# Adding up a node's counts where two groups of edges share it: TensorE products against GpSimd copies, and the order of the first loads, in a three-pass graph network kernel

## The chip, the cores and the metric

One core of one Trainium2 chip. The metric is the device time of one execution in microseconds (us). The kernel before takes 331.2 us, the median of 3 runs (330.82 to 331.33).

## What is computed

A graph of 3125 nodes with 128 features, and 53,125 edges `src -> dst` sorted by `dst`, each with one of 64 relation types. Three passes over the same edges, each of them a mean over the edges that end in a node:

```python
deg = segment_sum(ones, dst)
# 1: relation layer
msg = (x[src] + rel_emb[type]) @ W_msg.T + b_msg
x1  = layernorm(x + x @ W_self.T + b_self + segment_sum(msg, dst) / max(deg, 1))
# 2, 3: two SAGE layers
agg(h) = segment_sum(h[src], dst) / max(deg, 1)
h   = swish(agg(x1) @ W1_l.T + b1 + x1 @ W1_r.T)
out = layernorm(x1 + agg(h) @ W2_l.T + b2 + h @ W2_r.T)
```

## The kernel before

**The matrix of counts.** All three passes multiply node rows by one matrix `A` (`counts`), kept in SBUF as float16: 25 blocks of 128 source nodes (partitions) by 3150 target columns. The last block also holds, in its upper 64 partitions, how often each relation type ends in a node. Once `A` is there, each sum over edges is a row of dense products. The features are split into a high and a low float16 part, so that each block costs two products.

**Building it (the loop over groups).** The edges are cut into 416 tiles of 128, four tiles to a group, 104 groups. As the edges are sorted, a group touches a window of at most 38 columns, from its first target (`base`) on. For each group:

- VectorE writes the one-hot rows of the four tiles into one of three slots (L1386 for source row and type, L1393 for block and column), and every fourth group the rows for the types (`window_hot`, L1378) and for the node that is shared with the next group (`next_hot`, L1373). It may reuse a slot only when TensorE has counted the group three before (`released`).
- TensorE (`count`, L993) multiplies them into two PSUM banks, one for each half of the blocks: 8 products of 132 or 143 columns (L999) and 4 for the types (L1006). Two windows (`RING`) alternate, four banks in all.
- Two neighbouring groups mostly share a node: the last target of one is the first column of the next. The copy of the next window into `A` would overwrite that column. So TensorE multiplies the last tile of a group a second time into column 0 of the *next* window: `share(0)`, `share(1)` (L1016) and one product for the types (L1036), three for each group but the last. `share` waits until ScalarE has copied the group before out of that bank.
- ScalarE copies each half of the window to `A[:, half, base:base+38]` (L941), at an address from a register that it loads for eight groups at a time. A copy waits for the count and for the copy of the group before, since windows overlap.

**Work that rides along.** After the count of a group, TensorE does what is due by a table written out by hand: `project` (L1040, the nodes times `W_msg`, chunk c of 512 nodes after group `PROJECTED[c]`), `own` (L1121, the nodes times `W_self`, after the groups in `OWN`), and products of the first pass (`aggregate_tile`, L1079) for tiles of 128 nodes whose columns are complete. `spread()` deals these out: 13 products of 128 columns to a group, 16 up to group 15, 8 in the last four, none in groups of `OWN`, beginning with group `SUMS_FROM`. ScalarE and VectorE turn projected chunks into the two parts of the table (`high_bits` L854, `low_bits` L1403), and do the layer norm of finished chunks in turns spread over groups. VectorE also prepares the lists of groups 16 to 103 (`other_span`) between groups 8 and 15: eleven operations on 352 or 87 columns.

**Before the loop.** SyncE issues the loads of the edge lists (`dst`, `src`, for groups 0 to 15, then for 16 to 103), ScalarE those of `first_dst` and `type`. SyncE then waits for all targets before it issues `w_msg`, the biases and `x_turned` in three pieces (`CUTS`, chunks 0-1, 2-3, 4-6). TensorE runs 7 products on constants that nobody reads (`UNREAD`, L1186), then group 0.

**After it.** The rest of pass 1, then passes 2 and 3 by chunks of 512 nodes: 50 (or 49) products of 512 columns (L1101), `messages` (L1155), `own_later` (L1174), and the steps of ScalarE and VectorE behind them. The last chunk of pass 3 is one tile of 128 nodes. Its end is a chain: `lead` (L864), `messages`, `add_last` (L1480), `measure`, `combine`, `root`, `invert`, `normalise`, store. `keep_own` (L907) stands behind `root` of the chunk before on ScalarE. GpSimd writes constants at the start (L804 to L824) and then has nothing to do. Later, VectorE checks that the input meets the limits on which windows rely (`check_edges`), and a flag sends the rare other inputs to a slow general path.

## Time and profile before

| | us |
|---|---|
| median of 3 runs (range) | 331.2 (330.82 to 331.33) |
| the profiled execution | 331.4 |
| its span in the profile | 329.6 |
| loop over groups, first product to last | about 7.5 to 163.9 |
| rest of pass 1 | to about 175 |
| passes 2 and 3 | to about 327 |
| the last store | to the end |

The profile gives busy time of each engine, the chain of work that ended last, the costliest groups of instructions with their mean duration, and the order of instructions in time. VectorE, ScalarE and GpSimd instructions overlap with the next of the same engine by their last stretch, and TensorE's overlap far more: what one costs there is the step from its start to the next start, not its duration.

### The profile page before, as it was taken

The page shows a single profiled execution, that of the slowest core. Times are in us where ns is not written, and L with a number is a line of the kernel's source. Part 1 is how long each engine was busy: PE and PEld are TensorE (multiplying, and loading weights), DVE is VectorE, ACT ScalarE, POOL GpSimd, SP SyncE. Part 2 cuts the span into 40 slices and gives each one's busy share as a digit, 9 for nine tenths or more (in the row PEclk, how much of TensorE's full clock was granted, in tenths as well). Part 3 has the DMA queues.
Part 4 walks back from the last instruction along what each step waited for, and adds up shares of the span by engine and source line. Part 5 has one row for each costly group of instructions (what it writes and reads, how often), then busy time and mean ns, then how long its engine had stood idle before and what let it go on. Part 6 is the DMA issues. An engine that isn't in the chain of part 4 may idle for free.

```text
span 329.6 us, 10324 instructions
## 1 busy us (share of the span) xinstructions
PE 318.8 (97%) x3880; PEld 246.1 (75%) x3880; DVE 232.0 (70%) x632; ACT 167.4 (51%) x370; POOL 4.8 (1%) x20
## 2 busy tenths in 40 slices
PE   4899999999999999999999999999999999999994
PEld 1799999999999999999984554554564545545663
DVE  7699999999999999999777864314318246145154
ACT  4588777789789789788722322312322311211212
POOL 5000000000000000000000000000000000000000
PEclk9799999999999999999999999999999999999999
DMA  3500000000000000000011111111011112221111
GB/s 116 211 3 3 4 2 7 6 2 12 3 2 11 3 4 10 3 4 9 5 51 31 24 26 28 24 27 25 16 22 30 21 27 58 52 56 28 32 45 37
DMA packets 22087, 8.88 MB, mean 27 GB/s; under 512 B 16671, under 2 KB 21652, under 8 KB 22036
## 3 DMA queue, kind: packets, MB, share of 16 engines
q1 hardware_dynamic: 21460, 7.75, 9.6%
q8 instruction: 35, 0.57, 0.7%
q10 hardware_dynamic: 576, 0.43, 0.4%
q14 instruction: 16, 0.13, 0.1%
HBM read 3.02 MB, written 1.60 MB: 14 GB/s over the span
## 4 chain that ended last, share of the span: by engine, by line
PE 94%; DMA 3%; DVE 1%; SPq 1%; issue 0%; ACT 0%; DVEq 0%
PE ps L1101 39%; PE ps L1079 21%; PE ps L999 20%; PE ps L1174 4%; PE ps L1155 4%; PE ps L1051 2%; PE ps L1131 2%; PE ps L1006 1%; DMA counts<-dst_t 1%; DMA table<-x_turned 1%; PE ps L1016 1%; PE ps L1036 0%; DVE stats L1504 0%; PE ps L1115 0%; DVE new_first L1532 0%
## 5 line engine op out<-in xcount | busy, mean ns | idle before, releaser
L1101 PE MATMUL ps<-counts,table 128*128 128x512 f16 (+3 forms) x785 | 134.0, 329 | 0.0
L941 ACT CAST counts<-ps 128x494 f32 x208 | 107.0, 573 | 26.4 <-PE ps L999 25.6
L1101 PEld LDWEIGHTS ps<-counts,table 128*128 128x128 f16 x785 | 63.9, 97 | 65.1 <-issue 0.4
L1079 PE MATMUL ps<-table,counts 128*128 128x128 f16 x1200 | 81.9, 218 | 0.0
L1079 PEld LDWEIGHTS ps<-table,counts 128*128 128x128 f16 x1200 | 67.9, 97 | 0.0
L999 PE MATMUL ps<-hot 128*128 128x143 f16 (+1 forms) x560 | 60.2, 232 | 0.3 <-DVE hot L1393 0.3
L1393 DVE TENSOR_TENSOR hot<-iota,edges 128x1100 f16<-128x1100 f16 x70 | 50.5, 722 | 0.0
L999 PEld LDWEIGHTS ps<-hot 128*128 128x128 f16 x560 | 48.0, 100 | 2.3 <-DVE hot L1393 1.2
L1386 DVE TENSOR_TENSOR hot<-iota,edge_rows 128x768 f16<-128x768 f16 x70 | 38.4, 548 | 1.5 <-PE ps L1036 0.7
L1006 PE MATMUL ps<-window_hot,hot 128*128 128x19 f16 x280 | 38.8, 178 | 0.0
L884 ACT ACTIVATE scaled<-ps,rdeg 128x128 f32<-128x128 f32 (+1 forms) x74 | 21.4, 372 | 22.0 <-PE ps L1155 22.0
L1497 DVE TENSOR_TENSOR new_first<-ps,scaled 128x512 f32<-128x512 f32 (+2 forms) x9 | 5.7, 628 | 37.9 <-ACT scaled L884 37.9
L999 PE MATMUL ps<-room 128*128 128x132 f16 (+1 forms) x272 | 28.8, 231 | 0.0
L1006 PEld LDWEIGHTS ps<-window_hot,hot 128*128 128x128 f16 x280 | 27.4, 99 | 0.1
L1393 DVE TENSOR_TENSOR room<-iota,edges 128x1100 f16<-128x1100 f16 x34 | 24.6, 723 | 0.0
L1497 DVE TENSOR_TENSOR hot<-ps,scaled 128x512 f32<-128x512 f32 (+1 forms) x8 | 4.7, 583 | 27.5 <-ACT scaled L884 27.5
L999 PEld LDWEIGHTS ps<-room 128*128 128x128 f16 x272 | 23.5, 101 | 0.0
L864 ACT COPY room<-ps 128x512 f32<-128x512 f32 (+2 forms) x8 | 4.2, 524 | 32.5 <-PE ps L1101 32.4
L1016 PE MATMUL ps<-next_hot,hot 128*128 128x13 f16 (+1 forms) x138 | 19.4, 180 | 0.0
L1386 DVE TENSOR_TENSOR room<-iota,edge_rows 128x768 f16<-128x768 f16 x34 | 18.6, 548 | 0.3 <-PE ps L1036 0.2
L1006 PE MATMUL ps<-window_hot,room 128*128 128x19 f16 x136 | 18.8, 178 | 0.0
L864 ACT COPY hot<-ps 128x512 f32<-128x512 f32 (+2 forms) x8 | 3.6, 450 | 26.4 <-PE ps L1101 26.4
(146 smaller groups left out, 320.0 us busy)
## 6 DMA issues: line engine op xcount, KB each, us to landing
table<-x_turned SPq DMA_DIRECT2D x2, 512.0 KB, 4.3
edge_rows<-table SPq DMA_TRANSPOSE x54, 2.3
out<-new_first SPq DMA_DIRECT2D x3, 256.0 KB, 2.5
table<-x_turned SPq DMA_DIRECT2D x1, 576.0 KB, 5.7
out<-hot SPq DMA_DIRECT2D x2, 256.0 KB
window_hot<-table SPq DMA_TRANSPOSE x23, 2.4
iota<-table SPq DMA_TRANSPOSE x21, 2.3
counts<-counts SPq DMA_DIRECT2D x6, 53.0 KB
```

Source lines behind the costliest of these rows:

```text
L884: last = nc.scalar.activation(scaled[0:part, t], ps[0:part, bank, t * D:(t + 1) * D], ACT.Copy, scale=rdeg[0:part, tile:tile + 1])
L941: nc.scalar.copy(A[:, HALVES[half], bass.ds(bases[group % 8], GROUP_W)], window(group, half)).then_inc(copied[half], 1)
L999: return nc.tensor.matmul(window(group, half)[:, :, at[t]], row(tiles[t], LOW_AT, P), blocks_of(tiles[t], half), start=group == half == t ...
L1006: return nc.tensor.matmul(relations(group)[:, column], row(tiles[t], TYPE_AT, P), window_hot[:, group // NEXT % 2, tiles[t] // PAIR % (NEX ...
L1016: nc.tensor.matmul(window(then, half)[:, :, 0:1], row(tiles[-1], LOW_AT, P), next_hot[:, group // NEXT % 2, HALVES[half], group % NEXT].un ...
L1079: last = nc.tensor.matmul(ps[:, sums_bank(q), at:at + P], A[:, b, tile * P:(tile + 1) * P], table0[:, b, which, :], start=k == at == 0, st ...
L1101: last = nc.tensor.matmul(ps[:, sums_bank(q), 0:nodes], table[:, b, which, :], A[:, b, at:at + nodes], start=b == which == 0, stop=b + 1 = ...
L1155: sent = nc.tensor.matmul(ps[0:size, messages_bank(q), t * D:(t + 1) * D], sum_T(q)[:, at], weight(layer, 0), start=True, stop=True)
L1174: last = nc.tensor.matmul(to, x_T(q)[:, at], weight(layer, 1), start=q == EARLY and t == 0, stop=False, skip_group_check=True)
L1386: nc.vector.tensor_tensor(rows[:, :, TYPE_AT + REL_ROW:M_AT, :].rearrange("p h (k c) t -> p h k c t", c=PIECE), iota[:, 0:PIECE, :].unsque ...
L1393: nc.vector.tensor_tensor(rows[:, :, M_AT:M_AT + TILE_C, :], iota[:].unsqueeze(1).to_broadcast([P, PAIRS, TILE_C, PAIR]), edge[:, PLACED, ...
L1497: nc.vector.tensor_tensor(rows(new(q), q), from_own, rows(scaled, q), ALU.add).then_inc(y_ready, 1)
```

## The change

- GpSimd takes over the shared node. For each group from 1 on and each half it **saves** column `base` of `A` into `carried` before ScalarE's copy of that group overwrites it (`save`), and **adds** it back after (`add_carried`): four operations for each group, of 13 or 12 elements in each partition, with the address from a register (9 loaded at a time). ScalarE's copy now waits for `saved` instead of its own copy before. The products of the first pass wait for the additions too (`wait_shared`).
- TensorE's three products for the shared node go, with `next_hot`, `next_node` and `next_block` on VectorE. Count of group g now waits, ahead of its first product of each half, for the copies of group g-2. VectorE's slots come free with `counted[1]`.
- The first loads change order: lists of groups 0 to 15, `w_msg`, `x_turned` (pieces of chunks 0, 1-2, 3-6), biases, then the lists of groups 16 to 103, all on SyncE without the wait. ScalarE keeps the types of groups 16 to 103 after group 8 instead of ahead of the loop.
- `project(0)` goes ahead of group 0, the other chunks, the owns, the low bits and the first products of pass 1 come one group earlier, and 5 unread products stand in place of 7.
- At the end `keep_own` goes ahead of `root`, and the last of the three tiles of the chunk before is normalised by VectorE while it would wait for the last square root. The last chunk has its own column of the statistics for that.

The diff, cut to its core:

```diff
-PROJECTED = (1, 1, 2, 3, 4, 5, 6)
+PROJECTED = (-1, 0, 1, 2, 3, 4, 5)
 PROJECTED_BANKS = (4, 5, 6, 7)
-LOWS = {3: 0, 4: 1, 5: 2, 6: 3, 7: 4, 8: 5, 9: 6}
+LOWS = {2: 0, 3: 1, 4: 2, 5: 3, 6: 4, 7: 5, 8: 6}
 TURNING = 20
-CUTS = (0, 2, 4, 7)
-OWN = (7, 9, 11, 12, 14)
+CUTS = (0, 1, 3, 7)
+OWN = (6, 8, 10, 11, 13)
 OWN_BANKS = (7, 7, 6, 7, 6)
-SUMS_FROM, EARLY_STEPS = 8, 15
+SUMS_FROM, EARLY_STEPS = 7, 15
...
+OTHER_TYPES = 8
 LISTED = (slice(0, FIRST * GROUP), slice(FIRST * GROUP, TILES))
-UNREAD = 7
+UNREAD = 5
...
+        def wait_shared(eng, groups):
+            for half in range(2):
+                eng.wait_ge(copied[half], groups)
+                eng.wait_ge(shared[half], groups - 1)
...
-            for part, span in enumerate(LISTED):
-                sp.dma_start(dst_i[:, span], dst_t[:, span]).then_inc(dst_in[part], 16)
-                sp.dma_start(src_i[:, span], src_t[:, span]).then_inc(src_in[part], 16)
-            sp.wait_ge(dst_in[1], 32)
+            sp.dma_start(dst_i[:, LISTED[0]], dst_t[:, LISTED[0]]).then_inc(dst_in[0], 16)
+            sp.dma_start(src_i[:, LISTED[0]], src_t[:, LISTED[0]]).then_inc(src_in[0], 16)
             sp.dma_start(weights_first[:, 0, :], w_msg).then_inc(message_weights_in, 16)
-            for k, b in enumerate((b_self, b_msg)):
...
             for k, piece in enumerate(x_in):
                 span = slice(CUTS[k] * CHUNK, min(CUTS[k + 1] * CHUNK, BLOCKS * P))
                 sp.dma_start(stage[:, span], x_turned[:, span]).then_inc(piece, 16)
+            for k, b in enumerate((b_self, b_msg)):
+                sp.dma_start(bias_first[k:k + 1, 0, :], b).then_inc(biases_in, 16)
+            sp.dma_start(dst_i[:, LISTED[1]], dst_t[:, LISTED[1]]).then_inc(dst_in[1], 16)
+            others = slice(LISTED[1].start + GROUP, TILES)
+            sp.dma_start(first_i[:, others], first_dst[others].partition_broadcast(P)
+                         ).then_inc(dst_in[1], 16)
+            sp.dma_start(src_i[:, LISTED[1]], src_t[:, LISTED[1]]).then_inc(src_in[1], 16)
+            sp.dma_start(type_i[:, LISTED[1]], type_t[:, LISTED[1]]).then_inc(type_in[1], 16)
             sp.dma_start(weights_first[:, 1, :], w_self).then_inc(weights_in, 16)
             sp.dma_start(bias_first[:, 1, :], b1.rearrange("o d -> (o d)").partition_broadcast(P)
...
+            def node_of(column, half):
+                return A[:, HALVES[half], bass.ds(column, 1)]
+            def save(group, half, column):
+                pool.wait_ge(copied[half], group)
+                if half == 1 and group > 1:
+                    pool.wait_ge(shared[0], group - 1)
+                elif half == 1:
+                    pool.wait_ge(saved[0], group)
+                elif group > 2:
+                    pool.wait_ge(shared[1], group - 2)
+                elif group > 1:
+                    pool.wait_ge(saved[1], group - 1)
+                nc.gpsimd.tensor_copy(carried[:, group % 2, HALVES[half]].unsqueeze(2),
+                                      node_of(column, half)).then_inc(saved[half], 1)
+            def add_carried(group, half, column):
+                pool.wait_ge(copied[half], group + 1)
+                if group + 1 < GROUPS:
+                    pool.wait_ge(saved[half], group + 1)
+                elif half == 0:
+                    pool.wait_ge(shared[1], group - 1)
+                else:
+                    pool.wait_ge(shared[0], group)
+                node = node_of(column, half)
+                nc.gpsimd.tensor_tensor(node, node, carried[:, group % 2, HALVES[half]].unsqueeze(2),
+                                        ALU.add).then_inc(shared[half], 1)
+            pool.wait_ge(constants, 16)
+            pool.wait_ge(base_ready, 1)
+            for group in range(1, GROUPS):
+                if group == FIRST:
+                    pool.wait_ge(base_ready, 2)
+                if group % 8 == 1:
+                    begin = group - 1
+                    bases = nc.values_load_multi_w_load_instructions(
+                        base_i[0:1, begin:min(begin + 9, GROUPS)],
+                        engines=[mybir.EngineType.Pool], min_val=0, max_val=LAST_BASE,
+                        skip_runtime_bounds_check_because="they have been clipped")[1]
+                for half in range(2):
+                    save(group, half, bases[group - begin])
+                    if group > 1:
+                        add_carried(group - 1, half, bases[group - 1 - begin])
+            for half in range(2):
+                add_carried(GROUPS - 1, half, bases[GROUPS - 1 - begin])
             general_gpsimd(pool)
         @block.scalar
         def _(act):
-            for part, span in enumerate(LISTED):
-                begun = slice(span.start + GROUP * part, min(span.stop + GROUP, TILES))
-                act.dma_start(first_i[:, begun], first_dst[begun].partition_broadcast(P)
-                              ).then_inc(dst_in[part], 16)
-                act.dma_start(type_i[:, span], type_t[:, span]).then_inc(type_in[part], 16)
+            begun = slice(0, LISTED[0].stop + GROUP)
+            act.dma_start(first_i[:, begun], first_dst[begun].partition_broadcast(P)
+                          ).then_inc(dst_in[0], 16)
+            act.dma_start(type_i[:, LISTED[0]], type_t[:, LISTED[0]]).then_inc(type_in[0], 16)
...
-            for part, span in enumerate(LISTED):
+            def keep_types(part, span):
...
+                if 0 < q < ALL_CHUNKS - 1:
                     act.wait_ge(rows_ready, q)
-                nc.scalar.activation(std[0:part, 0:tiles_of(q)],
-                                     moments[0:part, 0:tiles_of(q), 1],
+                nc.scalar.activation(std[0:part, columns(q)], moments[0:part, columns(q), 1],
                                      ACT.Sqrt, bias=eps_col[0:part]).then_inc(std_ready, 1)
...
-                        act.wait_ge(copied[half], group)
+                        act.wait_ge(saved[half], group)
                     nc.scalar.copy(A[:, HALVES[half], bass.ds(bases[group % 8], GROUP_W)],
                                    window(group, half)).then_inc(copied[half], 1)
-                for c in range(CHUNKS):
+                for c in range(1, CHUNKS):
                     if PROJECTED[c] == group:
                         high_bits(c)
+                if group == OTHER_TYPES:
+                    keep_types(1, LISTED[1])
...
+                if q + 1 == ALL_CHUNKS:
+                    keep_own(q)
                 if layer_of(q - 1) == 1:
                     gate(q - 1)
                 else:
                     root(q - 1)
                 if layer_of(q - 1) < 2:
                     high(q - 1)
-                if q + 1 == ALL_CHUNKS:
-                    keep_own(q)
                 if ahead:
...
-                def share(half):
-                    if group:
-                        pe.wait_ge(copied[half], group)
-                    nc.tensor.matmul(
-                        window(then, half)[:, :, 0:1], row(tiles[-1], LOW_AT, P),
-                        next_hot[:, group // NEXT % 2, HALVES[half], group % NEXT].unsqueeze(2),
-                        start=True, stop=False, skip_group_check=True)
                 pe.wait_ge(v_hot, group + 1)
+                if group >= RING:
+                    pe.wait_ge(copied[0], group - RING + 1)
                 for t in range(GROUP):
                     last = blocks(0, t)
+                    if t == 0 and group >= RING:
+                        pe.wait_ge(copied[1], group - RING + 1)
                     if t + 1 < GROUP:
                         types(t)
...
-                if not ends:
-                    share(0)
                 blocks(1, 3).then_inc(counted[1], 1)
-                if not ends:
-                    share(1)
-                    nc.tensor.matmul(relations(then)[:, 0:1], row(tiles[-1], TYPE_AT, P),
-                                     next_node[:, group:group + 1], start=False, stop=False,
-                                     skip_group_check=True).then_inc(released, 1)
...
-                        wait_copied(pe, READY[tile])
+                        wait_shared(pe, READY[tile])
...
                         skip_runtime_bounds_check_because="they have been clipped")[1]
+                if group == 0:
+                    project(0)
                 mine = group % LOADED * GROUP
                 count(group, places[mine + 1:mine + GROUP])
-                for c in range(CHUNKS):
+                for c in range(1, CHUNKS):
                     if PROJECTED[c] == group:
                         project(c)
                 if group in OWN:
...
                 if group >= SLOTS:
-                    dve.wait_ge(released, group - SLOTS + 1)
+                    dve.wait_ge(counted[1], group - SLOTS + 1)
                 if group % NEXT == 0:
                     if group >= 2 * NEXT:
-                        dve.wait_ge(released, group - NEXT)
-                    nc.vector.tensor_tensor(
-                        next_hot[:, group // NEXT % 2],
-                        iota[:, P:P + BLOCKS, 0:1].to_broadcast([P, BLOCKS, NEXT]),
-                        next_block[:, group:group + NEXT].unsqueeze(1).to_broadcast(
-                            [P, BLOCKS, NEXT]), ALU.is_equal)
+                        dve.wait_ge(counted[1], group - NEXT)
...
                 dve.wait_ge(ln_step, 3 * normalised(q) + 1)
-                if q:
+                if 0 < q < ALL_CHUNKS - 1:
                     dve.wait_ge(rows_ready, q)
...
                     combine(q)
+                    if q + 1 == ALL_CHUNKS:
+                        normalise(q - 1, [tiles_of(q - 1) - 1])
                     invert(q)
-                    normalise(q, range(tiles_of(q)))
+                    normalise(q, range(tiles_of(q) - (q + 2 == ALL_CHUNKS)))
                 if layer_of(q) < 2:
```

## Rows read from the trace of the kernel before

**Rows 1.** The page: busy time, and the chain that ended last by engine.
```profile
PE 318.8 (97%) x3880; PEld 246.1 (75%) x3880; DVE 232.0 (70%) x632; ACT 167.4 (51%) x370; POOL 4.8 (1%) x20
...
PE 94%; DMA 3%; DVE 1%; SPq 1%; issue 0%; ACT 0%; DVEq 0%
```

**Rows 2.** Windows, the head and groups 17 to 99; clock, DMA share, GB/s last.
```profile
12.00:16.00 4.00, 4.00 (x33) 3.94 (x33) 2.48 (x6) 1.95 (x4) 0.00 (x0) 0.63 0.31 113
...
38.14:158.82 120.68, 120.65 (x2308) 119.58 (x2306) 115.72 (x275) 98.39 (x211) 0.00 (x0) 1.00 0.02 5
```

**Rows 3.** Timeline of TensorE: ends of groups 16, 98 and 99 (start, duration, what).
```profile
38.14 0.16 PE L1036 MATMUL ps<-next_node,hot 128*128 128x1 f16 x1
...
157.20 0.23 PE L999 MATMUL ps<-room 128*128 128x132 f16 x1
...
157.29 0.23 PE L999 MATMUL ps<-room 128*128 128x132 f16 x1
...
157.41 0.89 PE L1079 MATMUL ps<-table,counts 128*128 128x128 f16 x13
...
158.82 0.16 PE L1036 MATMUL ps<-next_node,hot 128*128 128x1 f16 x1
```

**Rows 4.** Timeline of VectorE in groups that nothing else interrupts.
```profile
66.66 0.55 DVE L1386 TENSOR_TENSOR room<-iota,edge_rows 128x768 f16<-128x768 f16 x1
67.12 0.72 DVE L1393 TENSOR_TENSOR room<-iota,edges 128x1100 f16<-128x1100 f16 x1
67.77 0.55 DVE L1386 TENSOR_TENSOR hot<-iota,edge_rows 128x768 f16<-128x768 f16 x1
...
68.96 0.23 DVE L1373 TENSOR_TENSOR next_hot<-iota,next_block 128x100 f16<-128x100 f16 x1
69.11 0.30 DVE L1378 TENSOR_TENSOR window_hot<-iota_type,edges 128x304 f16<-128x304 f16 x1
```

**Rows 5.** Timeline of the head: GpSimd's operations, and VectorE's beside them.
```profile
4.41 0.23 DVE L1282 TENSOR_TENSOR counts<-counts,base 128x64 int32<-128x64 int32 x1
...
4.60 0.10 POOL L814 MEMSET small<- 128x1 f32 x1
4.63 0.12 POOL L815 MEMSET degree<- 128x25 f32 x1
...
4.96 0.29 POOL L818 TENSOR_SCALAR_AFFINE_SELECT new_first<-new_first 128x128 f32<-128x128 f32 x1 [0.16 <-POOL peaks L816]
4.99 0.34 DVE L1310 TENSOR_TENSOR counts<-edges,place 128x64 int32<-128x64 f16 x1
```

**Rows 6.** Timeline of ScalarE: copies of two windows.
```profile
65.82 1.01 ACT L941 CAST counts<-ps 128x494 f32 x2 [0.42 <-PE ps L999]
```

**Rows 7.** Timeline of the head: unread products, first one-hots, wait for chunks 0 and 1.
```profile
4.06 3.17 PE L1186 MATMUL ps<-iota 128*128 128x512 f16 x7 [4.06 <-POOL iota L805]
...
6.28 0.55 DVE L1386 TENSOR_TENSOR hot<-iota,edge_rows 128x768 f16<-128x768 f16 x1
...
7.53 0.31 PE L999 MATMUL ps<-hot 128*128 128x143 f16 x1 [0.30 <-DVE hot L1393]
...
11.15 3.41 PE L1051 MATMUL ps<-weights_first,table 128*128 128x128 f32 x16 [1.46 <-DMA table<-x_turned]
```

**Rows 8.** Timeline of TensorE: chunk 3 projected at full clock.
```profile
17.03 1.14 PE L1051 MATMUL ps<-weights_first,table 128*128 128x128 f32 x8
```

**Rows 9.** Groups by line, VectorE, 16 to 38 us: low bits, first and last list operation.
```profile
L1403 DVE SCALAR_TENSOR_TENSOR table<-ps,table 128x512 f16<-128x512 f32 (+1 forms) x6 | 3.7, 614 | 0.0
...
L1282 DVE TENSOR_TENSOR counts<-counts,base 128x352 int32<-128x352 int32 x1 | 0.5, 518 | 0.0
...
L1278 DVE TENSOR_SCALAR base<-counts 128x87 int32<-128x87 int32 x1 | 0.2, 229 | 0.0
```

**Rows 10.** DMA issues: KB each, median us from issue to landing.
```profile
table<-x_turned SPq DMA_DIRECT2D x2, 512.0 KB, 4.3
```

**Rows 11.** Timeline of the end: ScalarE's copy ahead of the last chunk's messages.
```profile
324.37 0.27 ACT L864 COPY hot<-ps 128x128 f32<-128x128 f32 x1
```

67 lines of the change are left out of this document (24 added, 43 removed).

## The prediction

> **What bounds the kernel now.** I read the busy times and the chain first. TensorE is busy 97% of the span and 94% of the chain [rows 1]. The others only matter where they could take its place. The change touches the loop over groups, so next I read windows of it. Over 83 groups TensorE works 120.65 of 120.68 us, VectorE 115.72, ScalarE 98.39 and GpSimd nothing [rows 2]. So TensorE bounds the loop, but VectorE is only 4% behind it, and that decides this case. One group takes (158.82 - 38.14) / 83 = 1.454 us from the end of group 16 to that of 99 [rows 3]. VectorE, with its busy time taken whole, needs at most 115.72 / 83 = 1.394.
>
> In the head the bound is something else. TensorE stands still for 1.46 us until chunks 0 and 1 of `x_turned` arrive, and then works 3.41 us on 16 products [rows 7] that take about 2.1 at full clock (8 take 1.14, the run-out of the last among it, [rows 8]). The granted clock of 12 to 16 us is 0.63 of the full 2.4 GHz [rows 2], so part of that stretch ran at 1.2 GHz, behind that idle time.
>
> **1. TensorE's three products go.** A product costs the step to the next start. From L999 to L999 with a `share` between them it is 0.09 us, and from L999 over `share(1)` and L1036 to the first L1079 0.12 [rows 3]. Without them each is one step of 0.06, what a product of 132 columns leaves until the next start. That saves 0.03 + 0.06 = 0.09 a group. A group would take 1.454 - 0.09 = 1.365. The wait that comes in their place, for the copy of group g-2 at the start of group g, asks for less than `share` did: the same copy was due before the last product of group g-1, and now also the products of pass 1 lie in front of it. Price 0.
>
> **2. VectorE loses `next_hot`.** It costs 69.11 - 68.96 = 0.15 us in every fourth group [rows 4], 0.04 a group. VectorE then needs at most 1.394 - 0.04 = 1.357. The true need is some hundredths lower, since the busy time holds the last 0.08 of each operation, in which the next could have started (0.55 against a step of 0.46, [rows 4]). So VectorE's margin to TensorE's 1.365 is 0.01 to 0.05 us a group, and each of the four new GpSimd operations may delay it by about 0.01 before VectorE is the bound.
>
> **3. GpSimd's four operations a group.** GpSimd itself has time. The loop shows none of its operations, the head does: small memsets start 0.03 apart and last 0.10 to 0.12, one that reads and writes 128 columns lasts 0.29 [rows 5]. Four such, each behind a semaphore, make 0.5 to 1.2 us of 1.365. The register load for eight groups is one more stop in eight groups; it can run while GpSimd waits for ScalarE.
>
> ScalarE waits for `saved` in place of `copied`. Its two copies take 1.01 together and it stood idle 0.42 before them [rows 6]. The save of one half has the 0.5 us of the other half's copy to hide in. What is queued behind a late save is `add_carried` and the save of the other half, and who would wait is ScalarE's next copy, then TensorE's count two groups on. Behind 0.5 of cover and 0.4 of idle time I price it at 0. If the cover is gone, each half shows what a save is longer than 0.5.
>
> What it costs VectorE is the open term. Call it d for each operation. **Lower end: 0.** VectorE's step is 0.65 for 1100 columns and 0.46 for 768 [rows 4], so 0.19 / 332 = 0.57 ns a column, and 0.02 of each step (up to 0.07 with the rounding of these starts) is not for columns. A read of 13 elements may fit there. A gain is excluded, as GpSimd takes nothing from VectorE but the small `next_hot`, already counted. **Upper end: 0.11.** At 4.99 us L1310 took 0.34, where L1282 of as many columns took 0.23, and the one GpSimd operation that reads SBUF ran beside it, 4.96 to 5.25 [rows 5]. So a delay of VectorE behind GpSimd does exist here. That operation reads 128 columns, the new ones 13, and VectorE was let go about when it ended. I take d = 0.01: nearest in elements is the small memset, which leaves its engine after 0.03 [rows 5], and part of that falls into the free stretch of a step. Price in the loop: none while 4 x 0.01 fits the margin.
>
> The Trainium skill speaks against this change. "SBUF — State Buffer", section "Who interferes with whom", says that a VectorE instruction with two SBUF inputs contends with a GpSimd instruction that reads SBUF, and that the lock lasts for the whole instruction, whoever comes first. The L1310 row agrees in its direction; by that rule the sum would come out as the second rival below has it.
>
> **4. The head.** `project(0)` (about 1.0 us, [rows 8]) moves to where TensorE waits for the first one-hots. Five unread products of 0.45 end at 6.3, the first count started at 7.53 [rows 7]. It needs `w_msg` and one chunk of `x_turned`, issued at about 2 us instead of 7. The idle 1.46 goes, and the 1.3 that the low clock cost in 3.41. Together TensorE would save 3.8 us, more with 17 groups of 0.09, less 16 products of pass 1 that come earlier (0.9). VectorE is slower than that. From its first L1386, now at 6.28 [rows 7], 0.3 earlier without `next_hot` and two list operations, it has 17 groups of 1.11 (67.77 - 66.66, [rows 4]), five `window_hot` of 0.22, seven low bits of 0.6 or less and nine list operations from 0.5 to 0.2 [rows 9], in all 18.9 + 1.1 + 4.0 + 3.2 = 27.2 us, so group 16 is ready at 33.3, counted at 34.0. I add 0.8 for waits between the two and 0.7 for 17 x 4 x 0.01. So group 16 ends at 35.5 where it ended at 38.14 [rows 3]: **-2.6**. Bounds: 0 if the loads come late, -4.1 if VectorE never waits.
>
> The moved loads: SyncE issues all of them, past one wait less. The lists of groups 16 to 103 now stand behind 1.6 MB of `x_turned`, but VectorE wants them in group 8, near 20 us. `w_self` stands last and is wanted in group 4. The types' two operations on ScalarE move into its idle time in group 8. Price 0 each.
>
> **5. The loop from group 17 on.** 87 groups less 0.09: **-7.7**. VectorE does chunk work in bursts, with three slots to even them out, and the margin is thin. I give back **+1.0** (0 to 3).
>
> **6. The end.** ScalarE's `lead` of the last chunk started at 324.37 behind `keep_own` [rows 11] and would start about 0.1 earlier, and one tile less stands ahead of `add_last` on VectorE. Each is a step on the last chain: **-0.2**. The store of the chunk before goes out some tenths later, still ahead of the last store.
>
> **Sum**, against the profiled execution's own 331.4 (span 329.6 and 1.8 around it; the median of the runs is 331.2, 0.2 lower): 331.4 - 2.6 - 7.7 + 1.0 - 0.2 = 321.9, and **322.0** for the median as far as this can tell.
>
> **Rivals.**
> *d near 0.03, about even.* VectorE becomes the bound. With d = 0.024, (1.454 - 1.357) / 4, the loop is as long as before. At 0.035, the memsets' distance, it is 1.497 x 87, +3.7, and the head -3.3 + 2.4: 331.4 + 3.7 - 0.9 - 0.2 = 334. This holds 326 to 336, either side of no change.
> *Slower: VectorE and GpSimd take turns at SBUF.* One mechanism, at L1386 and L1393: each reads two inputs from SBUF, and GpSimd's save or add holds it off, or waits itself until it ends and lets ScalarE's next copy wait. It decides from d = 0.024 on. At 0.06, half of what L1310 lost, a group takes 1.60: 87 x 0.14 + 0.8 - 0.2 gives 344. At 0.11, 1.80: 87 x 0.34 + 4.2 gives 365. I would expect 350. For it: L1310, and that VectorE is busy nearly always, so that no operation of GpSimd can avoid it. Against it: 13 elements are a tenth of what that row read.
> *The loads don't come in time.* `x_turned` took 4.3 us from issue [rows 10] for two chunks. If one chunk came after 6.3, TensorE would idle and again run at 1.2 GHz, and the head would give nothing: 325.
>
> **Chances.** Forecast 0.48, even 0.20 (0.08 faster, 0.04 the same, 0.08 slower), turns 0.25, late loads 0.07. "Same" is within 0.2%, 0.7 us, about what a measurement of this kernel can tell. That makes faster 0.63, same 0.04, slower 0.33. The range: from 318.5 (head -4.1, nothing given back, VectorE at its lower need) over the even case to 344, the near end of the turns. The forecast's own range is 319 to 325.
>
> **What would show it.** Right: a group from 17 to 99 takes 1.36 to 1.39, no row of L1016, L1036 or L1373, VectorE near 97% busy, L1386 still 0.55 and L1393 still 0.72, no TensorE wait for L941 or GpSimd, no low clock in the head. Wrong: L1386 or L1393 longer than before, or steps between them longer, TensorE waiting for VectorE's one-hots (d over 0.01), GpSimd's operations lasting many tenths, ScalarE's copies waiting for GpSimd. The head is wrong if TensorE waits for `x_turned` or shows 1.2 GHz after 7.5 us.

## The result, and the profile after

The changed kernel takes **398.8 us** (median of 4 runs, 397.98 to 399.01), against 331.3 before: a ratio of 1.2035, 95% interval 1.1997 to 1.2073. It is 67.5 us slower. I had forecast 322, with 344 as the upper end. Medians in this text are over all runs of a kernel; ratios and their intervals leave out the few executions that stood more than 1.5% above the fastest of the same kernel.

The page of the changed kernel, busy time, the chain that ended last by engine, and ScalarE's copies; then GpSimd's two groups in the loop (42 to 221 us):

```profile
PE 350.3 (88%) x3569; PEld 258.0 (65%) x3569; DVE 233.3 (59%) x601; ACT 177.4 (45%) x370; POOL 143.0 (36%) x432
...
PE 41%; POOL 35%; issue 16%; POOLq 6%; DVE 1%; ACT 0%; DVEq 0%; ACTq 0%
...
L1005 ACT CAST counts<-ps 128x494 f32 x208 | 117.6, 568 | 87.0 <-POOL carried L855 79.2
```
```profile
L868 POOL TENSOR_TENSOR counts<-counts,carried 128x12 f16 (+1 forms) x166 | 62.0, 374 | 26.9 <-POOL carried L855 5.5
L855 POOL COPY carried<-counts 128x13 f16 (+1 forms) x165 | 49.2, 298 | 40.9 <-POOL counts L868 40.9
```

Before, the chain was 94% TensorE [rows 1]. Now GpSimd, its sequencer and "issue" hold 57% of it. ScalarE stood idle 79 us in all behind the saves (L855). In the loop GpSimd's 62.0 + 49.2 us of work and 26.9 + 40.9 us between its own operations make 179.0 of 179 us: it never waits for anybody else there, and its own chain is the bound. VectorE is busy as long as before, over a longer span: it is not what got slower.

Windows of the changed kernel: the loop, its last part, and what follows (clock, DMA share, GB/s last):

```profile
38.00:200.00 162.00, 134.83 (x1836) 117.40 (x1837) 103.94 (x227) 95.59 (x188) 101.19 (x301) 0.96 0.01 4
200.00:230.00 30.00, 24.46 (x346) 22.55 (x343) 18.06 (x40) 18.06 (x37) 18.11 (x58) 0.89 0.01 4
230.00:396.00 166.00, 160.07 (x1068) 91.51 (x1065) 78.31 (x260) 40.20 (x104) 1.21 (x6) 0.99 0.15 33
```

I time the loop by where the last product of a group's count starts (L1064 here). Group 16 is there at 41.02 us (38.03 before), group 99 at 221.38 (158.73). A group takes 2.173 us instead of 1.454, 83 x 0.719 = 59.7 us more. The rest of the 65.2 by which group 103 is late is the head's 3.0 and 2.5 in the last four groups. Behind the loop it needs 1.4 us more (167.1 against 165.7 from group 103 to the end). The granted clock is 0.96 and 0.89 of full in the windows where TensorE is busy 83% and 82%. As GpSimd's chain has no pause in the loop, that clock doesn't set the pace there.

GpSimd's timeline in the loop, where nothing holds it up and where VectorE does:

```profile
101.19 0.20 POOL L855 COPY carried<-counts 128x13 f16 x1 [0.22 <-POOL counts L868]
101.54 0.24 POOL L868 TENSOR_TENSOR counts<-counts,carried 128x13 f16 x1
102.01 0.20 POOL L855 COPY carried<-counts 128x12 f16 x1 [0.23 <-POOL counts L868]
102.35 0.25 POOL L868 TENSOR_TENSOR counts<-counts,carried 128x12 f16 x1
102.83 0.20 POOL L855 COPY carried<-counts 128x13 f16 x1 [0.22 <-POOL counts L868]
...
105.51 0.60 POOL L868 TENSOR_TENSOR counts<-counts,carried 128x13 f16 x1
```

From 101.19 to 102.83 four operations take 1.64 us with VectorE out of the way. That is one group, and already more than the 1.454 of a group before. 0.20 and 0.25 of each pair is work, 0.15 and 0.22 is the way from the end of one operation over its semaphore to the start of the next. Ahead of each save it holds an operation on the address register (FUSED_REGOPS, 0.046). Where the addresses are fixed (e5 below), the same two ways take 0.08 and 0.13. The add at 105.51 takes 0.60, as VectorE's L1412 runs from 105.46.

VectorE beside them, the groups of the loop (42 to 221 us):

```profile
L1419 DVE TENSOR_TENSOR hot<-iota,edges 128x1100 f16<-128x1100 f16 x55 | 40.3, 732 | 0.0
L1412 DVE TENSOR_TENSOR hot<-iota,edge_rows 128x768 f16<-128x768 f16 x54 | 30.1, 557 | 19.0 <-PE ps L1064 18.9
```

0.732 and 0.557 stand against 0.72 and 0.55 [rows 4]: VectorE lost 0.01 an operation, and waits for TensorE.

### The profile page after: what moved, and what is told of

It is laid out like the page before. It is cut to its first block, busy times and chain, and to the rows that moved or that the text cites. A ratio compares the mean times of both kernels' runs of the same rounds, so it can differ in the third digit from the quotient of the medians.

```text
span 396.2 us, 10862 instructions
## 1 busy us (share of the span) xinstructions
PE 350.3 (88%) x3569; PEld 258.0 (65%) x3569; DVE 233.3 (59%) x601; ACT 177.4 (45%) x370; POOL 143.0 (36%) x432
## 4 chain that ended last, share of the span: by engine, by line
PE 41%; POOL 35%; issue 16%; POOLq 6%; DVE 1%; ACT 0%; DVEq 0%; ACTq 0%
PE ps L1154 33%; POOL counts L868 18%; POOL carried L855 16%; PE ps L1227 3%; PE ps L1208 3%; POOLq L855 2%; POOLq L878 2%; POOLq L862 1%; POOL iota L819 1%; PE ps L1132 1%; PE ps L1104 1%; PE ps L1239 1%; POOLq L852 0%; POOLq L848 0%; POOLq L868 0%
## 5 line engine op out<-in xcount | busy, mean ns | idle before, releaser
L1005 ACT CAST counts<-ps 128x494 f32 x208 | 117.6, 568 | 87.0 <-POOL carried L855 79.2
L1132 PE MATMUL ps<-table,counts 128*128 128x128 f16 x1200 | 87.6, 227 | 6.8 <-ACT counts L1005 4.1
L868 POOL TENSOR_TENSOR counts<-counts,carried 128x13 f16 x206 | 76.8, 373 | 33.4 <-POOL carried L855 6.7
L1132 PEld LDWEIGHTS ps<-table,counts 128*128 128x128 f16 x1200 | 75.7, 102 | 9.4 <-ACT counts L1005 4.1
L855 POOL COPY carried<-counts 128x13 f16 x206 | 61.2, 297 | 54.8 <-POOL counts L868 49.9
L1064 PE MATMUL ps<-hot 128*128 128x143 f16 (+1 forms) x560 | 73.9, 242 | 2.1 <-DVE hot L1419 0.9
L1071 PE MATMUL ps<-window_hot,hot 128*128 128x19 f16 x280 | 44.8, 182 | 17.4 <-ACT counts L1005 17.0
L1064 PEld LDWEIGHTS ps<-hot 128*128 128x128 f16 x560 | 49.6, 101 | 8.0 <-DVE hot L1419 2.0
L1412 DVE TENSOR_TENSOR hot<-iota,edge_rows 128x768 f16<-128x768 f16 x70 | 39.0, 557 | 21.9 <-PE ps L1064 21.6
L1064 PE MATMUL ps<-room 128*128 128x132 f16 (+1 forms) x272 | 36.4, 247 | 0.6 <-DVE hot L1419 0.4
L1071 PE MATMUL ps<-window_hot,room 128*128 128x19 f16 x136 | 22.1, 186 | 8.8 <-ACT counts L1005 8.5
L1064 PEld LDWEIGHTS ps<-room 128*128 128x128 f16 x272 | 24.5, 104 | 3.3 <-issue 0.7
L1412 DVE TENSOR_TENSOR room<-iota,edge_rows 128x768 f16<-128x768 f16 x34 | 18.9, 557 | 11.4 <-PE ps L1064 11.4
L1071 PEld LDWEIGHTS ps<-window_hot,room 128*128 128x128 f16 x136 | 14.0, 103 | 12.4 <-ACT counts L1005 12.1
```

What stands on the lines that cost most here:

```text
L855: nc.gpsimd.tensor_copy(carried[:, group % 2, HALVES[half]].unsqueeze(2), node_of(column, half)).then_inc(saved[half], 1)
L868: nc.gpsimd.tensor_tensor(node, node, carried[:, group % 2, HALVES[half]].unsqueeze(2), ALU.add).then_inc(shared[half], 1)
L1005: nc.scalar.copy(A[:, HALVES[half], bass.ds(bases[group % 8], GROUP_W)], window(group, half)).then_inc(copied[half], 1)
L1064: return nc.tensor.matmul(window(group, half)[:, :, at[t]], row(tiles[t], LOW_AT, P), blocks_of(tiles[t], half), start=half == t == 0, sto ...
L1071: return nc.tensor.matmul(relations(group)[:, column], row(tiles[t], TYPE_AT, P), window_hot[:, group // NEXT % 2, tiles[t] // PAIR % (NEX ...
L1132: last = nc.tensor.matmul(ps[:, sums_bank(q), at:at + P], A[:, b, tile * P:(tile + 1) * P], table0[:, b, which, :], start=k == at == 0, st ...
```

## The experiments

Two theories. **A:** GpSimd's four operations are one serial chain of 1.64 us a group, on which ScalarE's next copy hangs. VectorE's one-hots make it longer. **B:** taking turns with VectorE at SBUF is the loss. "Loop" is a group from 16 to 99 as above, in the profiled execution; "save" and "add" are the mean durations in the loop (of the operations in their place for e5 and e8, of 25 elements for e6's add). e2, e7, e8, e9 and e11 were run once each.

| kernel | time, us | loop, us | save, add, us |
|---|---|---|---|
| before | 331.3 | 1.454 | |
| changed | 398.8 | 2.173 | 0.298, 0.374 |
| e1 rest only | 328.8 | 1.455 | |
| e2 no one-hots | 360.1 | 1.797 | 0.211, 0.270 |
| e4 loose chain | 350.7 | 1.682 | 0.398, 0.448 |
| e7 loose, no one-hots | 318.7 | 1.368 | 0.204, 0.248 |
| e9 VectorE writes only | (loop alone) | 1.805 | 0.219, 0.266 |
| e5 beside | 331.3 | 1.454 | 0.413, 0.455 |
| e8 beside, writes only | 331.2 | 1.455 | 0.112, 0.113 |
| e6 three operations | 337.8 | 1.548 | 0.444, 0.542 |
| e11 saves only | 339.2 | 1.536 | 0.418 |
| e10 half each | 334.6 | 1.495 | 0.482, 0.446 |
| e12 half each, a pause | 333.9 | 1.453 | 0.414, 0.353 |

**e1: the rest of the change alone.** Against the changed kernel, shortened:

```diff
-                        act.wait_ge(saved[half], group)
+                        act.wait_ge(copied[half], group)
...
+                if not ends:
+                    share(0)
...
+                if not ends:
+                    share(1)
+                    nc.tensor.matmul(relations(then)[:, 0:1], row(tiles[-1], TYPE_AT, P),
+                                     next_node[:, group:group + 1], start=False, stop=False,
+                                     skip_group_check=True).then_inc(released, 1)
```

`save`, `add_carried` and the waits on `shared` are gone too, and VectorE makes `next_hot` again.

> All of the change but GpSimd's part: loads, project(0) ahead of group 0, tables one group earlier and the end as in the changed kernel, TensorE's three products for the shared node as before. Both theories say the 67 us belong to GpSimd's part, so this must be faster than the kernel before. The prediction priced head and end at -2.8 us with the one-hots 0.3 earlier; with next_hot kept: 328 to 329 us, a group still 1.45 us. If the head also costs something (group 16 ends 3 us later in the changed kernel), it is at 331 or more.

328.77 us (ratio 0.992, 0.989 to 0.995), as both theories had it. Group 16 is there at 35.64, 2.4 earlier than before, and the loop is unchanged. So the loss is GpSimd's part, and this version is the one that beats both kernels. The head's timeline shows why: `project` of chunk 0 stands ahead of the first count, and no product waits for `x_turned`:

```profile
4.46 1.91 PE L1199 MATMUL ps<-iota 128*128 128x512 f16 x4
6.54 1.79 PE L1064 MATMUL ps<-weights_first,table 128*128 128x128 f32 x8 [0.16 <-issue]
8.16 0.23 PE L1012 MATMUL ps<-hot 128*128 128x143 f16 x1
...
175.70 2.54 PE L1114 MATMUL ps<-counts,table 128*128 128x512 f16 x11
```

Chunk 0's eight products take 1.79 us where eight took 1.14 [rows 8]. The window of 6.5 to 8.3 us says a granted clock of 1.00, but the trace holds no record of the clock before 7.92. The starts of the products tell: the unread ones of 512 columns follow each other at 0.43 (4.89, 5.32, 5.75), those behind the loop (L1114) at 0.215. Chunk 0's products follow at 0.21 up to 7.94 and at 0.11 from there on. So TensorE ran at the lower of its two levels, 1.2 GHz, from its first product at 4.06 to about 7.9, and chunk 0 fell into that stretch.

**e2: no one-hots on VectorE** from group 3 on; one small memset stands in their place, and TensorE multiplies old rows, so the counts are not those of the graph.

```diff
+                if group >= SLOTS:
+                    nc.vector.memset(rows[:, :, M_AT:M_AT + 1, :], 0.0).then_inc(v_hot, 1)
+                    return
```

> The changed kernel, with VectorE's one-hots left out from group 3 on (one small memset in their place; TensorE multiplies old rows). GpSimd's chain is untouched, VectorE hardly reads SBUF in the loop. Theory A (GpSimd's own serial chain, 0.82 us for a half with no VectorE beside it, bounds the loop, and VectorE's one-hots only add to it): the save falls from 0.297 to 0.20 mean and the add from 0.373 to 0.25, a group takes 1.64 us instead of 2.17, 354 us in all. Theory B (taking turns with VectorE is all of the loss): a group falls to what TensorE needs, 1.37, and the time to about 325.

360.1 us, where A said 354 and B 325. GpSimd's operations in the loop (37 to 184 us):

```profile
L868 POOL TENSOR_TENSOR counts<-counts,carried 128x12 f16 (+1 forms) x164 | 44.3, 270 | 26.6 <-POOL carried L855 5.7
L855 POOL COPY carried<-counts 128x13 f16 (+1 forms) x163 | 34.4, 211 | 42.1 <-POOL counts L868 41.7 <-ACT counts L1005 0.4
```

Both are back at nearly their undisturbed length. Work and ways of GpSimd again fill all 147 us. B fails as the only cause: with VectorE out of the way a group takes 1.80, far over TensorE's 1.37. A is a little off too, 1.80 for 1.64: the ways are 0.16 and 0.26 in the mean, and a few operations still meet one of VectorE's remaining ones. The changed kernel's loop is 0.38 longer than this one: that is VectorE's part, 31 us in 83 groups.

**e4: the loose chain.** GpSimd waits only for what it needs.

```diff
-                if half == 1 and group > 1:
-                    pool.wait_ge(shared[0], group - 1)
-                elif half == 1:
-                    pool.wait_ge(saved[0], group)
-                elif group > 2:
-                    pool.wait_ge(shared[1], group - 2)
-                elif group > 1:
-                    pool.wait_ge(saved[1], group - 1)
+                if group > 2:
+                    pool.wait_ge(shared[half], group - 2)
...
-                if group + 1 < GROUPS:
-                    pool.wait_ge(saved[half], group + 1)
-                elif half == 0:
-                    pool.wait_ge(shared[1], group - 1)
-                else:
-                    pool.wait_ge(shared[0], group)
+                pool.wait_ge(saved[half], group)
```

> The changed kernel, but GpSimd waits only for what it needs: a save for ScalarE's copy and for the add that last used its slot, an add for the copy and for its own save three operations back, no longer for the operation right ahead. Theory A: the gap of 0.12 to 0.22 us ahead of each operation shrinks, about 0.1 off each of four, a group at 1.75 us and 360 us in all. Theory B: the turns with VectorE remain and set the pace, 2.1 us a group and 390 or more.

350.7 us (1.0545 to 1.0624 of before), 48 us faster than the changed kernel by these waits alone. So the chain was the larger part. It went below A's 360, because operations that don't wait for each other can start 0.16 after the one ahead, before that one has ended:

```profile
101.55 0.19 POOL L849 COPY carried<-counts 128x12 f16 x1
101.71 0.56 POOL L857 TENSOR_TENSOR counts<-counts,carried 128x12 f16 x1
102.18 0.70 POOL L849 COPY carried<-counts 128x13 f16 x1
...
103.00 0.19 POOL L849 COPY carried<-counts 128x12 f16 x1
103.16 0.24 POOL L857 TENSOR_TENSOR counts<-counts,carried 128x12 f16 x1
```

**e7: both gone.** e4 and e2 together, the one-hots left out as there.

> The loose chain with VectorE's one-hots left out from group 3 on (one small memset in their place; TensorE multiplies old rows): both costs of GpSimd's part gone, its serial chain and VectorE's turns. If these two are all that the prediction missed, a group takes the 1.365 us that TensorE needs without its three products, and the whole the predicted 320 to 324. If a third cost is left (register loads, ScalarE's wait for saves), it stays over 330.

318.7 us, a group 1.368. TensorE's part of the forecast (1.365) holds to 0.003 us, and no third cost of size is left. ScalarE's waits in this loop are for TensorE's counts again (11.4 us, against 2.4 for saves, between 34 and 150 us).

**e5 and e8: beside the kernel before.** Nobody waits for these operations; each waits for the one ahead, at fixed addresses. e8 has a memset of the same part of `spare` in place of each. e5's, shortened:

```diff
+                    nc.gpsimd.tensor_copy(spare[...], fixed[...]).then_inc(spared, 1)
+                    pool.wait_ge(spared, done + 1)
+                    nc.gpsimd.tensor_tensor(spare[...], spare[...], fixed[...], ALU.add
+                                            ).then_inc(spared, 1)
```

> The kernel before, with the same four GpSimd operations a group (copy and add of 13 or 12 elements, chained as in the changed kernel, on buffers of their own at fixed addresses), for which nobody waits. It measures d, what one of them costs VectorE. Theory A and B: VectorE wins the turns, L1386 and L1393 are longer by 0.01 us as in the changed kernel, the time is 331 to 333, and GpSimd's operations last 0.3 to 0.37 in the mean beside 0.20 to 0.25 alone. If GpSimd won turns (the prediction's rival with d of 0.06), 344.

> As the run beside, but both operations are memsets of 13 or 12 elements: GpSimd writes SBUF and reads nothing. If it is GpSimd's reads that meet VectorE's second input, each lasts about 0.10 us as alone in the head, never 0.3 or more. If any use of SBUF by GpSimd meets VectorE, they lasts 0.3 in the mean as the copies did. The whole takes 331 in either case.

e5 takes 331.3 (ratio 1.0001, 0.998 to 1.002): **d, the delay of VectorE, doesn't show in the time.** VectorE has 0.06 us a group to spare there, and its one-hots are longer by 0.006 at most. The delay is on the other side. GpSimd, for which nobody waits, can't keep up: four of its operations take 2.17 us, as long as a group of the changed kernel, so that 222 of the 412 fall into the loop and the last starts at 207 us. GpSimd's operations in e5's loop, then in e8's (20 to 160 us):

```profile
L839 POOL TENSOR_TENSOR spare<-spare,fixed 128x13 f16<-128x13 f16 (+1 forms) x130 | 59.1, 455 | 10.4
L835 POOL COPY spare<-fixed 128x12 f16<-128x12 f16 (+1 forms) x129 | 53.3, 413 | 17.4 <-POOL spare L839 0.5
```
```profile
L838 POOL MEMSET spare<- 128x12 f16 (+1 forms) x189 | 21.4, 113 | 10.9
L835 POOL MEMSET spare<- 128x13 f16 (+1 forms) x188 | 21.1, 112 | 86.2 <-ACT counts L957 85.9
```

With reads 0.41 and 0.46 us, about twice the 0.20 and 0.25 of e7, and more than the 0.30 to 0.37 expected. With writes alone 0.11, as in the head [rows 5].

**e9: VectorE writes only.** The changed kernel, its one-hots replaced by memsets of the same tiles from group 3 on.

```diff
+                if group >= SLOTS:
+                    nc.vector.memset(rows[:, :, TYPE_AT + REL_ROW:M_AT, :], 0.0)
+                    nc.vector.memset(rows[:, :, M_AT:M_AT + TILE_C, :], 0.0).then_inc(v_hot, 1)
+                    return
```

> The changed kernel (chain as it is), with VectorE's two one-hot operations replaced from group 3 on by memsets of the same tiles (counts are zero then): VectorE is about as busy, but reads no SBUF there. If two SBUF inputs on VectorE are what GpSimd waits for, the copies last 0.20 and the adds 0.25 us and a group takes 1.80 as without one-hots, 360 us. If a busy VectorE is enough, a group takes 2.1 to 2.2 and the whole 395.

Counts are zero then, the flag sends the kernel to its general path, and the whole time (22 ms) says nothing. The loop ran first and can be read: VectorE's memsets, and GpSimd beside them.

```profile
L1414 DVE MEMSET hot<- 128x550 uint32 x54 | 27.9, 517 | 3.4
L1413 DVE MEMSET hot<- 128x384 uint32 x54 | 20.4, 378 | 19.0 <-PE ps L1064 18.1
```
```profile
L868 POOL TENSOR_TENSOR counts<-counts,carried 128x12 f16 (+1 forms) x164 | 43.7, 266 | 26.6 <-POOL carried L855 5.7
L855 POOL COPY carried<-counts 128x12 f16 (+1 forms) x164 | 36.0, 219 | 42.3 <-POOL counts L868 42.0 <-ACT counts L1005 0.4
```

A group takes 1.805, as without one-hots, with VectorE busy 62% of the loop (64% in the changed kernel). So it is VectorE's reads that GpSimd's reads meet, and neither side's writes. That they are reads of two inputs the traces show one by one: in this loop 22 of GpSimd's 330 operations are over 0.1 us longer than alone, and 21 of them met one of the operations with two inputs that VectorE still has there (`window_hot`, `new_first`, `table`); one met a copy. Over the loops of all runs with copies and adds of 12 or 13 elements, 58 of these met nothing but `BATCH_NORM_STATS2`, which reads one input, and none lasted over 0.005 us longer. "SBUF — State Buffer" of the Trainium skill, "Who interferes with whom", states that a VectorE instruction with two SBUF inputs contends with a GpSimd instruction that reads SBUF, and not with one that only writes it; e5, e7, e8 and e9 agree.

**e6, e11: fewer operations.** Against the changed kernel, on top of the loose waits: one add of 25 elements for both halves, and four slots for what is carried (e6), or no adds (e11, counts of shared nodes missing):

```diff
+            def add_carried(group, column):
+                for half in range(2):
+                    pool.wait_ge(copied[half], group + 1)
+                    pool.wait_ge(saved[half], group)
+                node = node_of(column, slice(0, BLOCKS))
+                nc.gpsimd.tensor_tensor(node, node, carried[:, group % 4, :].unsqueeze(2),
+                                        ALU.add).then_inc(shared[0], 1)
```
```diff
                 for half in range(2):
                     save(group, half, bases[group - begin])
-                    if group > 1:
-                        add_carried(group - 1, half, bases[group - 1 - begin])
```

> The loose chain (350.7 us), with one add of 25 elements for both halves behind the two saves, and four slots for what is carried: three GpSimd operations a group instead of four. There GpSimd was busy 0.40 + 0.43 us for each half, 1.66 a group, and a group took 1.68. Theory A2 (GpSimd's rate, each operation prolonged by the VectorE operation that it meets, is the bound of that kernel): 2 x 0.40 + 0.45 = 1.25 a group, so ScalarE and TensorE come in, a group at 1.45 and 330 us. Theory B2 (the wait of ScalarE for each save is the bound, however many adds there are): a group stays at 1.6 or more, 345.

> The loose chain with its four operations cut to the two saves a group; the adds are left out, so that counts of shared nodes are missing. What three operations left open (337.8 us, a group 1.55) is whether the saves' own wait or the adds between them hold ScalarE. If the adds (GpSimd's rate): a group at 1.40, 322 us. If a save that meets a VectorE operation is enough by itself: 1.5 or more, 334.

337.8 us (1.0138 to 1.0252) fell between A2 (330) and B2 (345). With four operations GpSimd's rate did count: it was busy 125.5 of 142 us in e4, and the three operations and two more slots of e6 take 0.134 us a group off. From there on it is the saves: with the adds gone altogether (e11) a group still takes 1.536 against e6's 1.548. e11's whole is longer, 339.2, as a save of 4.00 us in the head makes it late there (group 16 at 39.10, in e6 at 34.48). What is left is ScalarE's wait for single saves that meet VectorE at the wrong time.

**e10: a version meant to win,** and **e12.** TensorE keeps `share(0)` for the first half, GpSimd has the second, with the loose waits. Against the kernel before, the part in the loop:

```diff
-                        act.wait_ge(copied[half], group)
+                        act.wait_ge(saved if half else copied[0], group)
...
-                if not ends:
-                    share(1)
-                    nc.tensor.matmul(relations(then)[:, 0:1], row(tiles[-1], TYPE_AT, P),
-                                     next_node[:, group:group + 1], start=False, stop=False,
-                                     skip_group_check=True).then_inc(released, 1)
```

> A version meant to beat both: the rest of the change, with TensorE's share(0) for the first half of the blocks as before, and GpSimd's save and add for the second half and the types alone, waiting only for what they need. TensorE drops share(1) and L1036, 0.06 us a group; GpSimd has two operations a group instead of four, and ScalarE's second copy has the first one's 0.5 us and its idle time to cover the save. Theory A (GpSimd's rate and chain were the loss): a group at 1.40 us, 87 x 0.055 + 17 x 0.055 = 5.7 us less than the rest of the change alone (328.8): 323. If even one save a group holds up ScalarE and TensorE, a group stays at 1.45 or more and it is at 329 or more.

334.6 us, spread over 330.8 to 338.3, where 323 was hoped for: a miss, and slower than before (ratio 1.0033 to 1.0103). The profiled execution was one of the shortest, 331.95. Half of its groups take 1.40 or less, as expected. But three saves in the loop lasted 2.8 to 3.0 us. GpSimd, and VectorE at the same time:

```profile
61.14 3.05 POOL L849 COPY carried<-counts 128x12 f16 x1 [0.69 <-ACT counts L991]
64.15 0.24 POOL L856 TENSOR_TENSOR counts<-counts,carried 128x12 f16 x1
```
```profile
60.72 0.54 DVE L1437 TENSOR_TENSOR hot<-iota,edge_rows 128x768 f16<-128x768 f16 x1
61.19 0.72 DVE L1444 TENSOR_TENSOR hot<-iota,edges 128x1100 f16<-128x1100 f16 x1
61.83 0.55 DVE L1437 TENSOR_TENSOR hot<-iota,edge_rows 128x768 f16<-128x768 f16 x1
62.30 0.72 DVE L1444 TENSOR_TENSOR hot<-iota,edges 128x1100 f16<-128x1100 f16 x1
62.94 0.55 DVE L1437 TENSOR_TENSOR room<-iota,edge_rows 128x768 f16<-128x768 f16 x1
63.41 0.72 DVE L1444 TENSOR_TENSOR room<-iota,edges 128x1100 f16<-128x1100 f16 x1
```

A copy of 12 elements stands from 61.14 to 64.19. VectorE's row of one-hots, each issued before the last had ended, runs to 64.13. ScalarE stood idle 2.57 us for it.

In e12 VectorE waits for its own last one-hot once a group, against e10:

```diff
+                if group:
+                    dve.wait_ge(v_hot, group)
```

> Half by TensorE, half by GpSimd as before (334.6 us, spread over 330.8 to 338.3), and VectorE waits once a group for the end of its own last one-hot before it issues the next. In the half-each kernel three of GpSimd's saves lasted about 3 us (61.14 to 64.19), as long as VectorE's one-hots followed each other without a pause, and ScalarE waited 2.6 us for one. Theory C (GpSimd gets its turn only when VectorE's queue of SBUF readers has a pause): no save over 0.8 us is left, a group takes 1.40 to 1.44, VectorE's step grows by 0.07 a group, 325 to 329 us with a small spread. If a pause on VectorE doesn't let GpSimd in, saves of 3 us stay and the time is 334 or more.

333.9 us, 333.6 to 334.7 in four runs: the spread is small as expected, but the 325 to 329 are missed. In the loop one save lasted 1.01 us and no other over 0.83: the long ones are gone there. In the head, where list operations stand between the one-hots and VectorE has no pause at the wait, the longest of all is seen:

```profile
26.84 5.18 POOL L849 COPY carried<-counts 128x12 f16 x1 [1.51 <-ACT counts L991]
31.99 0.24 POOL L856 TENSOR_TENSOR counts<-counts,carried 128x12 f16 x1
```

Group 16 is at 40.54 us, against 35.64 in e1. The loop takes 1.453: the pause costs VectorE about 0.1 a group (60.04 to 60.79 for a step of 0.64), and with it VectorE is busy 116.9 of 119 us and bounds the loop. The loop of one profiled execution and the small spread speak for theory C (no save over 1.01 us in 83 groups, three of about 3 us in e10's 83); a pause of another length was not tried. The remedy is worth nothing here.

## Why the prediction was wrong

**Step 3, GpSimd's four operations, failed, at the words "I price it at 0".** Three sizes in it were wrong.

- *The chain.* I took 0.10 to 0.29 an operation from memsets and one wide operation, "0.5 to 1.2 us of 1.365" in all. A copy takes 0.20, an add 0.25, and each waits 0.15 to 0.22 for the one right ahead: 1.64. I had read in the code that each waits for its predecessor, and did not price the way there and back. e4 against the changed kernel: 0.49 us a group, 48 us in all.
- *The turns, from the wrong side.* I asked what GpSimd costs VectorE (d) and let that decide. d was small as I had it: I took 0.01 for each of the four, and the two one-hots of a group grew by 0.01 each, which is 0.005 for each of the four; e5 shows nothing in the time. The delay of GpSimd behind VectorE, which the second rival names in half a sentence, had no term in the sum. It is 0.10 to 0.12 an operation in the changed kernel and 0.20 when the chain is loose. e2 against the changed kernel: 0.38 us a group, 31 to 39 us in all.
- *The cover.* "The save of one half has the 0.5 us of the other half's copy to hide in" holds for an undisturbed save (e7), but not where one stands for 0.7 or 3 us (e11, e10).

The two parts nearly add up: 2.173 - 0.491 - 0.376 = 1.306, measured 1.368 with both gone (e7), which is what TensorE needs and so the least that could be seen. My signs of being wrong named what came: GpSimd's operations of several tenths, and ScalarE's copies waiting for GpSimd.

**The second rival** had the right sign and place and a chance of 0.25. Its price of 344 to 365 came from d, so it too was 34 us short of 398.8. The rule of the Trainium skill ("SBUF — State Buffer", "Who interferes with whom") pointed the right way, and I discounted it by the argument that 13 elements are short. For the one who waits, what counts is how long the *other* side's operation is: 0.55 and 0.72 us.

**Step 1** is right: e7's loop of 1.368 stands against 1.365, and e7's 318.7 under my 322 is what VectorE no longer costs in the head (group 16 at 32.35, not 35.5). **Step 2**, VectorE's need of 1.357, was never put to the test: no run has all of its one-hots without `next_hot` and without GpSimd beside them.

**Step 4, the head:** -2.6 predicted, -2.4 measured in e1 (35.64 against 38.03), which keeps `next_hot`. Chunk 0 came in time. Its products took 1.79 us in place of the 1.0 I took, as TensorE was still at 1.2 GHz. The unread products had shown it: seven took 3.17 us [rows 7], 0.43 a step, twice a step at full clock. The count of group 0 starts 0.24 after its one-hots are ready (8.16 against 7.92), and that costs nothing, since VectorE bounds the head as I had it: it is busy 22.57 of 22.60 us from 13 to 35.6. In the changed kernel GpSimd's chain turned the gain into +3.0. Up to group 5 that kernel is 0.7 us ahead of e1, from there to group 16 a group takes 2.22 us. VectorE's list operations come on top from 20.4 us on.

**Step 5** was a term for an unbroken loop, and nothing of it is left in the changed kernel. **Step 6, the end:** -0.2 predicted. From group 103 to the end of the span e1 takes 165.5 and the kernel before 165.7.

**Chances and range.** 0.63 for faster rested on a sum in which the new waits cost nothing. The low end of 318.5 doesn't come out of its own terms: 331.4 - 4.1 - 7.7 - 0.2 is 319.4, as TensorE's 1.365 stays the floor of the loop whatever VectorE needs. The range ended at 344 because I took the near end of the rival's range, whose far end stood on VectorE's loss, not on the chain's.

## What to carry to other kernels

Where a step moves to another engine, write its chain down as a loop (operation, way to the next wait, operation) and compare that with the period of the loop that it joins, before asking what it costs anyone else. A short GpSimd operation that reads SBUF beside a VectorE full of two-input operations has no length of its own (0.20 us alone, 0.41 in the mean and up to 5.18 here): let nothing on the critical path wait for it, and let it wait only for what it needs.

## What the runs showed of the hardware that I had not expected

- GpSimd can be shut out, not merely delayed by one operation: 3.05 us behind six unpaused VectorE operations (e10) and 5.18 us behind some thirteen (e12); e11 has three of 2.90 to 4.00. Mostly it gets in after one, and what decides between the two is open.
- The delay is one-sided in this mix: VectorE's operations grew by 0.01 us at most, GpSimd's doubled (e5). In the head of the changed kernel, an operation of GpSimd that met a running VectorE operation was the one to be late (L832 took 0.36), where before GpSimd was first and VectorE lost 0.11 [rows 5]:

```profile
4.96 0.23 DVE L1352 TENSOR_TENSOR counts<-edges,place 128x64 int32<-128x64 f16 x1
4.98 0.36 POOL L832 TENSOR_SCALAR_AFFINE_SELECT new_first<-new_first 128x128 f32<-128x128 f32 x1 [0.17 <-POOL peaks L830]
```
- GpSimd memsets of 13 elements last 0.11 us, copies 0.20 and adds 0.25, undisturbed. Dependent ones cost 0.15 to 0.22 more each (0.08 to 0.13 at fixed addresses, e5), independent ones can start 0.16 apart.
- A granted clock of 1.00 in a window can mean that there is no record for it. TensorE took 0.43 a step for the unread products of 512 columns from 4.06 us on, and 0.215 for such a product behind the loop, both at a "1.00" (e1): compare steps of the same product before ruling the clock out.
